# Gathers that add in their buffer: the source rows of an edge-to-node kernel, from group 4 on

## The chip, the cores and the metric

The kernel runs on one core of a Trainium2 chip. The metric is the device time of one launch in microseconds. The kernel before takes 477.14 us, the median of three runs (476.47 to 477.19). A difference of 0.2%, some 0.95 us, is about what a measurement of this kernel can tell from no change.

## The reference

A graph has 50,000 nodes with 128 features each (`x`) and 25,000 edges, sorted by their target. Each edge brings a message, the positive part of its source's row plus its own features. The messages of a node are summed, a two-layer network runs on every node, and a layer norm ends it. All is float32.

```python
msg = relu(x[src] + edge_attr)                     # 25,000 x 128
agg = segment_sum(msg, dst, num_segments=50000)
h = x + agg
h = relu(relu(h @ W1 + b1) @ W2 + b2)              # W1 128x256, W2 256x128
out = layernorm(x + h)                             # over the 128 features, eps 1e-5
```

## The kernel before

The nodes are cut into 131 groups, numbered 0 to 130, of 384 nodes (3 tiles of 128); the last has 80. To each group belongs a window of 256 edges (two chunks of 128), whose start is worked out on the chip from the sorted targets. Groups 0 to 3 are started by hand in halves; from group 4 on every group goes the same way, and the text speaks of those.

The path of the edges of group g:

- SyncE (its queue is SP) loads the edge features of the window into `pre_msg`, slot g % 6 (line 109, 128 KB). `load_ea` first reads the window's start from SBUF into a register, and waits until the slot's last reader, `low_part(g - 6)`, is done.
- GpSimd (POOL) issues two gathers, one for each chunk, each of 128 rows of `x` (64 KB) into `x_src`, slot g % 6 (line 115). They wait for the copy `hT_copied` of group g - 4 (line 559). Behind the gathers of group g POOL normalizes the third tile of group g - 8 (`third_tile`, line 549).
- VectorE (DVE) adds `x_src` to `pre_msg` in place (`add_edge_attr`, line 609), then tells ScalarE by `sum_ready`. It waits for the edge features in the middle of `aggregate` (line 661) and for the gathers just before the addition (line 608).
- ScalarE (ACT) makes the rounded positive part, `high_part` (line 765), VectorE the remainder, `low_part` (line 616), and TensorE adds both to the group's sum by four matmuls with the 0/1 matrix `sel` (line 886).

The path of the nodes: TensorE turns x into the same bank (line 859), ScalarE copies the sum (`hT`, line 771), TensorE and ScalarE run the network (lines 922, 777, 930), VectorE adds bias and x (lines 632, 646) and makes the statistics (653, 662, 668, 673), and ScalarE (796) and POOL (549) write the normalized tiles.

Every engine's order is written out by hand, with semaphores between the engines. In DVE's turn g: add_bias(g), low_part(g+2), add_x(g), reciprocal(g-2), statistics(g), shifts(g-2), select(g+3), aggregate(g), add_edge_attr(g+3). In ACT's turn g high_part(g+2) comes after copy_hT(g+1) and one normalized tile. SyncE's own turn g is what the prediction follows most:

```python
load_x(g + X_AHEAD)      # X_AHEAD = 5; waits for z of group g - 1
load_ea(g + EA_AHEAD)    # EA_AHEAD = 5; waits for low_part of group g - 1
store(g - 4)             # waits for ACT's tiles and for POOL's third_tile(g - 4)
```

SyncE runs these in order, so a store that waits holds up the next loads.

Of the kernel before, what the change touches and what calls it, by code (L numbers as in the profile page):

```python
# [7 lines left out]
ALU = mybir.AluOpType  # L8
# [31 lines left out]
EB, XB, ZB, YB, SB = 6, 6, 8, 6, 8  # L40
# [2 lines left out]
EA_FIRST, EA_AHEAD = 2, 5  # L43

FIRST_CHUNKS = 4
PARTS = {g: [slice(0, 1), slice(1, 2)] for g in range(4)}
WHOLE = {0: 0, 2: 1, 3: 2}
FLAGS = 9
# [2 lines left out]
def partitions(g, c):  # L51
    return LP if g == c["LAST"] else 128


def tiles(g, c):
    return LT if g == c["LAST"] else T


def windows(g, c):
    return 1 if g == c["LAST"] else K  # L60


def parts(g, c):

    return PARTS.get(g, [slice(0, windows(g, c))])


def parts_to(g, c):

    return sum(len(parts(i, c)) for i in range(g))  # L70
# [7 lines left out]
def loads_to(slot, g):  # L78

    return 16 * len(range(slot, g + 1, EB))  # L80


def gathers_to(slot, g, c):

    return 16 * sum(windows(i, c) for i in range(slot, g + 1, EB) if i >= 4)
# [26 lines left out]

def start_gather(nc, x, g, k, loaded, c):
    index = c["last_pairs"][:, 0:1] if g == c["LAST"] else c["src_of"][:, g - FIRST_ROW, k:k + 1]
    nc.gpsimd.indirect_dma_start(  # L115
        out=c["x_src"][:, g % EB, k, :], out_offset=None, in_=x,
        in_offset=bass.IndirectOffsetOnAxis(ap=index, axis=0)).then_inc(loaded, 16)


def start_windows(nc, pairs, c):  # L120
# [45 lines left out]
def prepare(nc, x, edge_attr, dst, pairs, w1, b1, w2, b2, c, sb, sem):  # L166
# [113 lines left out]
    def link(dve, ins):  # L280

        chain[0] += 1
        ins.then_inc(vec, 1)
        dve.wait_ge(vec, chain[0])
# [52 lines left out]
    def prepare_vector(dve):  # L337
# [4 lines left out]
        link(dve, nc.vector.memset(most[:, :], FAR))  # L342
        nc.vector.memset(most[0:1, :], float(FIRST_CHUNKS * EW))

# [47 lines left out]
    def prepare_scalar(act):  # L392
# [4 lines left out]
                      allow_slow_non_contiguous=True).then_inc(next_loaded, 16)  # L397
        act.dma_start(first_pairs[:, 1:FIRST_CHUNKS, :], pairs[EW:FIRST_CHUNKS * EW, :].rearrange("(k p) a -> p k a", p=EW),
                      allow_slow_non_contiguous=True).then_inc(more_pairs_loaded, 16)
# [37 lines left out]
def main_path(nc, x, pairs, edge_attr, out, c, sb, sem, checks):  # L437
# [17 lines left out]
    x_sb, pre_msg, x_loaded, ea_loaded = c["x_sb"], c["pre_msg"], c["x_loaded"], c["ea_loaded"]  # L455

    x_src, sel, end_sel, last_sel = c["x_src"], c["sel"], c["end_sel"], c["last_sel"]
# [14 lines left out]
    xsrc_loaded, sel_ready = c["xsrc_loaded"], c["sel_ready"]  # L472
    out_stored = c["out_stored"]
    targets_ready = sem("targets_ready")
    sum_ready = sem("sum_ready")
# [21 lines left out]
    def inside(g):  # L497

        return 0 <= g < GROUPS
# [44 lines left out]
    def main_gpsimd(pool):  # L544
        def third_tile(g):

            pool.wait_ge(shift_ready, g + 1)
            pool.wait_ge(out_stored[g % YB], (g // YB) * 16)
            nc.gpsimd.tensor_scalar(y[:, g % YB, 2, :], z[:, g % ZB, 2, :], rstd[:, g % SB, 2:3], shift[:, g % SB, 2:3],  # L549
                                    ALU.mult, ALU.add).then_inc(y_tile_ready, 1)  # L550

        pool.wait_ge(c["src_of_ready"], 1)
        for g in (2, 3):
            for k in range(K):
                start_gather(nc, x, g, k, c["first_loaded"][2 * g + k], c)
        for g in range(4, GROUPS):
            back = g - GATHER_AHEAD
            if inside(back):
                pool.wait_ge(hT_copied, back + 1)
            if g == LAST:  # L560
                pool.wait_ge(c["last_pairs_loaded"], 16)
            for k in range(windows(g, c)):
                start_gather(nc, x, g, k, xsrc_loaded[g % EB], c)
            if POOL_FROM <= g - POOL_BACK:
                third_tile(g - POOL_BACK)
        for g in range(GROUPS - POOL_BACK, LAST - 3):
            third_tile(g)

        for g, ts in ((LAST - 3, range(T)), (LAST - 2, (2,)), (END, (1, 2))):
            pool.wait_ge(shift_ready, g + 1)  # L570
            pool.wait_ge(out_stored[g % YB], (g // YB) * 16)
            for t in ts:
                last = nc.gpsimd.tensor_scalar(y[:, g % YB, t, :], z[:, g % ZB, t, :], rstd[:, g % SB, t:t + 1],
                                               shift[:, g % SB, t:t + 1], ALU.mult, ALU.add)
            last.then_inc(y_pool_ready, 1)

    def main_vector(dve):
# [18 lines left out]
        def edge_attr_there(g):  # L596

            dve.wait_ge(ea_loaded[g % EB], loads_to(g % EB, g))

        def add_edge_attr(g, i=0):  # L600

            ks = parts(g, c)[i]
            if g < 4:
                edge_attr_there(g)
            if g < 4:
                dve.wait_ge(c["first_loaded"][2 * g + i], 16 * (ks.stop - ks.start))
            else:
                dve.wait_ge(xsrc_loaded[g % EB], gathers_to(g % EB, g, c))
            nc.vector.tensor_tensor(pre_msg[:, g % EB, ks, :], pre_msg[:, g % EB, ks, :], x_src[:, g % EB, ks, :],  # L609
                                    ALU.add).then_inc(sum_ready, 1)  # L610

# [14 lines left out]
        def add_bias(g):  # L626

            p, n = partitions(g, c), tiles(g, c)
            if g == 0:
                dve.wait_ge(c["b2_loaded"], 16)  # L630
            dve.wait_ge(h2_summed, g + 1)
            nc.vector.tensor_tensor(h2[0:p, g % 2, 0:n, :], h2_ps[g % 2][0:p, 0:n, :], b2_sb[0:p, :, :].to_broadcast([p, n, D]),  # L632
                                    ALU.add).then_inc(h2_ready, 1)
# [22 lines left out]
        def aggregate(g):  # L656
            p = partitions(g, c)
            dve.wait_ge(stats_ready, g + 1)
            for t in range(tiles(g, c)):
                if t == 1 and g >= 1 and inside(g + 3):  # L660
                    edge_attr_there(g + 3)
                last = nc.vector.bn_aggr(mean_var[0:p, g % SB, t, :], stats[0:p, g % SB, t, :])
            last.then_inc(var_ready, 1)

        def reciprocal(g):
            p, n = partitions(g, c), tiles(g, c)
            dve.wait_ge(std_ready, g + 1)
            nc.vector.reciprocal(rstd[0:p, g % SB, 0:n], std[0:p, g % SB, 0:n]).then_inc(rstd_ready, 1)

        def shifts(g):  # L670
            p, n = partitions(g, c), tiles(g, c)
            dve.wait_ge(rstd_ready, g + 1)
            nc.vector.scalar_tensor_tensor(shift[0:p, g % SB, 0:n], mean_var[0:p, g % SB, 0:n, 0], -1.0, rstd[0:p, g % SB, 0:n],  # L673
                                           ALU.mult, ALU.mult).then_inc(shift_ready, 1)
# [40 lines left out]
        statistics(1)  # L715
        select(4)
        aggregate(1)
        add_edge_attr(4)
        for g in range(2, LAST):
            if g == END:  # L720
                for done in (g - 2, g - 1):
                    reciprocal(done)
                    shifts(done)
            add_bias(g)
            if inside(g + 2):
                low_part(g + 2)
            add_x(g)
            if inside(g - 2) and g < END:
                reciprocal(g - 2)
            statistics(g)  # L730
            if inside(g - 2) and g < END:
                shifts(g - 2)
            z_free(g + 1)
            if inside(g + 3):
                select(g + 3)
            aggregate(g)
            if inside(g + 3):
                add_edge_attr(g + 3)
            if g in TARGETS_FOUND:
                checks["find_targets"](dve, TARGETS_FOUND.index(g))  # L740
            if g == TARGETS_CHECKED:
                checks["check_targets"](dve)
            if g == CHECKED + 1:
                checks["set_general"](dve)
# [10 lines left out]
    def main_scalar(act):  # L755
# [5 lines left out]
        def high_part(g, i=0):  # L761

            ks = parts(g, c)[i]
            act.wait_ge(sum_ready, parts_to(g, c) + i + 1)
            nc.scalar.activation(msg_hi[:, g % EB, ks, :], pre_msg[:, g % EB, ks, :], ACT.Relu).then_inc(msg_hi_ready, 1)  # L765

        def copy_hT(g):
# [431 lines left out]
def gnn_resnorm_kernel(nc, x, dst, pairs, edge_attr, w1, b1, w2, b2, out, h_dram):  # L1199
# [9 lines left out]
    with ctx:  # L1209
        def sb(name, shape, dt=FP32):  # L1210
            return ctx.enter_context(nc.sbuf_tensor(name, shape, dt))
# [4 lines left out]
        def sem(name):  # L1216
# [14 lines left out]
            node_row=sb("node_row", [128, K + 1, R]),  # L1231
            first_pairs=sb("first_pairs", [EW, FIRST_CHUNKS, 2], INT32),
            first_dst=sb("first_dst", [EW, FIRST_CHUNKS]),
            last_pairs=sb("last_pairs", [EW, 2], INT32),
# [3 lines left out]
            last_sel=sb("last_sel", [EW, LP], FP32R),  # L1238
            second_sel=sb("second_sel", [EW, FIRST_CHUNKS - 1, T * 128], FP32R),
            first_sel=sb("first_sel", [EW, K, T * 128], FP32R),  # L1240
# [106 lines left out]
```

## Time and profile before

| | us |
|---|---|
| median of 3 runs | 477.14 |
| time of the profiled execution | 474.89 |
| its span, first to last instruction | 473.0 |
| TensorE busy | 457.9 (97% of the span) |
| VectorE busy | 434.3 (92%) |
| ScalarE busy | 395.7 (84%) |
| GpSimd busy | 365.7 (77%) |
| mean granted clock of TensorE, of full speed | 0.993 |

The profiled execution lies 2.25 us under the median. Busy time counts instructions in work, not waits; DMA issues on SyncE don't count. POOL's spans are rough. A releaser named "issue" means that the engine waited for nothing that the profile shows.

### The profile page before, as it was taken

The page shows a single profiled execution, that of the slowest core. Times are in us where ns is not written, and L with a number is a line of the kernel's source. Part 1 is how long each engine was busy: PE and PEld are TensorE (multiplying, and loading weights), DVE is VectorE, ACT ScalarE, POOL GpSimd, SP SyncE. Part 2 cuts the span into 40 slices and gives each one's busy share as a digit, 9 for nine tenths or more (in the row PEclk, how much of TensorE's full clock was granted, in tenths as well). Part 3 has the DMA queues.
Part 4 walks back from the last instruction along what each step waited for, and adds up shares of the span by engine and source line. Part 5 has one row for each costly group of instructions (what it writes and reads, how often), then busy time and mean ns, then how long its engine had stood idle before and what let it go on. Part 6 is the DMA issues. An engine that isn't in the chain of part 4 may idle for free.

```text
span 473.0 us, 10533 instructions
## 1 busy us (share of the span) xinstructions
PE 457.9 (97%) x3033; PEld 378.0 (80%) x3033; DVE 434.3 (92%) x1761; ACT 395.7 (84%) x924; POOL 365.7 (77%) x403
## 2 busy tenths in 40 slices
PE   7879999999999999999999999999999999999994
PEld 5657888888888888888888888888888888888883
DVE  5658999999999999999999999999999999999996
ACT  2349888888888989888988888888889898888885
POOL 6546888888877776787888888888888888888843
PEclk9989999999999999999999999999999999999998
DMA  5625666666667676666666666666666666666632
GB/s 131 178 75 174 185 197 192 197 194 196 195 179 208 180 207 182 209 180 195 192 199 191 196 196 193 199 190 196 194 196 190 200 187 202 186 198 188 198 110 87
DMA packets 83613, 86.80 MB, mean 184 GB/s; under 512 B 11767, under 2 KB 79252, under 8 KB 83556
## 3 DMA queue, kind: packets, MB, share of 16 engines
q1 hardware_dynamic: 74388, 68.76, 46.3%
q0 software_dynamic: 8496, 17.38, 14.2%
q8 instruction: 23, 0.38, 0.4%
q14 instruction: 34, 0.28, 0.2%
q10 hardware_dynamic: 672, 0.00, 0.1%
HBM read 60.51 MB, written 25.60 MB: 182 GB/s over the span
## 4 chain that ended last, share of the span: by engine, by line
PE 95%; DVE 1%; another core or an unknown queue 1%; ACT 1%; issue 0%; DMA 0%; DVEq 0%
PE h_ps L930 37%; PE h1T_ps L922 36%; PE hT_ps L886 12%; PE hT_ps L859 9%; PE h1T_ps L413 1%; DMA dst_first<-in_dst_dram 0%; ACT h1T L777 0%; PE prep_ps L423 0%; ACT hT L771 0%; DVE h L632 0%; DVE stats L653 0%; ACT std L782 0%; DVE z L646 0%; PE prep_ps L912 0%
## 5 line engine op out<-in xcount | busy, mean ns | idle before, releaser
L115 POOL DMA_INDIRECT x_src<-in_x_dram,src_of x256 | 269.4, 1052 | 84.8 <-issue 58.0
L930 PE MATMUL h_ps<-w_sb,h1T 128*128 128x128 f32 x1564 | 197.9, 276 | 1.8 <-issue 1.6
L922 PE MATMUL h1T_ps<-hT,w_sb 128*128 128x384 f32 (+1 forms) x524 | 191.6, 488 | 3.7 <-ACT hT L771 3.7
L777 ACT ACTIVATE h1T<-h1T_ps,b_sb 128x384 f32<-128x384 f32 (+1 forms) x262 | 151.7, 580 | 50.7 <-issue 32.7
L930 PEld LDWEIGHTS h_ps<-w_sb,h1T 128*128 128x128 f32 x1564 | 185.5, 192 | 2.6 <-issue 2.1
L922 PEld LDWEIGHTS h1T_ps<-hT,w_sb 128*128 128x128 f32 x524 | 89.9, 192 | 39.0 <-ACT hT L771 3.5
L796 ACT ACTIVATE y<-z,shift,rstd 128x128 f32<-128x128 f32 x261 | 113.6, 482 | 0.6 <-DVE shift L673 0.5
L632 DVE TENSOR_TENSOR h<-h_ps,b_sb 128x384 f32<-128x384 f32 x131 | 72.7, 555 | 25.6 <-PE h_ps L930 14.7
L549 POOL TENSOR_SCALAR y<-z,rstd,shift 128x128 f32<-128x128 f32 x123 | 85.1, 692 | 13.6 <-DVE shift L673 9.1
L653 DVE BATCH_NORM_STATS2 stats<-z 128x6 f32<-128x128 f32 x391 | 88.7, 282 | 0.1
L859 PEld LDWEIGHTS hT_ps<-ident,x_sb 128*128 128x128 f32 (+1 forms) x379 | 49.5, 142 | 39.6 <-issue 22.8
L592 DVE TENSOR_TENSOR sel<-node_in_range,dst_of 128x432 fp32r<-128x432 f32 x127 | 76.2, 600 | 0.0
L646 DVE SCALAR_TENSOR_TENSOR z<-h,x_sb 128x384 f32<-128x384 f32 x131 | 72.1, 550 | 0.0
L886 PE MATMUL hT_ps<-sel,msg_hi 128*128 128x216 f32 x250 | 71.2, 310 | 0.1
L771 ACT ACTIVATE hT<-hT_ps 128x384 f32<-128x384 f32 x128 | 62.6, 489 | 1.7 <-PE hT_ps L900 1.4
L886 PE MATMUL hT_ps<-sel,msg_lo 128*128 128x216 f32 x250 | 62.3, 276 | 0.0
L859 PE MATMUL hT_ps<-ident,x_sb 128*128 128x128 f32 (+1 forms) x379 | 62.1, 272 | 0.0
L765 ACT ACTIVATE msg_hi<-pre_msg 128x256 fp32r<-128x256 f32 (+1 forms) x132 | 54.3, 412 | 8.6 <-DVE pre_msg L609 4.5
L616 DVE SCALAR_TENSOR_TENSOR msg_lo<-pre_msg,msg_hi 128x256 fp32r<-128x256 f32 (+1 forms) x132 | 54.1, 410 | 4.6 <-ACT msg_hi L765 4.4
L609 DVE TENSOR_TENSOR pre_msg<-pre_msg,x_src 128x256 f32<-128x256 f32 (+1 forms) x135 | 57.7, 428 | 0.4 <-DMA x_src<-in_x_dram,first_pairs 0.4
L886 PEld LDWEIGHTS hT_ps<-sel,msg_hi 128*128 128x128 f32 x250 | 47.7, 191 | 0.4 <-DVE msg_lo L616 0.4
L886 PEld LDWEIGHTS hT_ps<-sel,msg_lo 128*128 128x128 f32 x250 | 48.0, 192 | 0.0
(133 smaller groups left out, 182.8 us busy)
## 6 DMA issues: line engine op xcount, KB each, us to landing
x_sb<-in_x_dram SPq DMA_DIRECT2D x130, 192.0 KB
out_dram<-y SPq DMA_DIRECT2D x130, 192.0 KB
pre_msg<-in_edge_attr_dram SPq DMA_DIRECT2D x130, 128.0 KB
x_src<-in_x_dram,src_of POOLq DMA_INDIRECT x256
w_sb<-in_w_dram SPq DMA_DIRECT2D x2, 128.0 KB
dst_rows<-in_dst_dram SPq DMA_DIRECT2D x1, 97.7 KB
x_src<-in_x_dram,first_pairs POOLq DMA_INDIRECT x4, 2.7
b_sb<-in_b_dram SPq DMA_DIRECT2D x1, 64.0 KB, 3.1
```

The costliest lines, as they stand in the source:

```text
L115: nc.gpsimd.indirect_dma_start(out=c["x_src"][:, g % EB, k, :], out_offset=None, in_=x, in_offset=bass.IndirectOffsetOnAxis(ap=index, axis ...
L549: nc.gpsimd.tensor_scalar(y[:, g % YB, 2, :], z[:, g % ZB, 2, :], rstd[:, g % SB, 2:3], shift[:, g % SB, 2:3], ALU.mult, ALU.add).then_inc ...
L592: nc.vector.tensor_tensor(sel[:, g % EB, :, :], node_in_range[:, :, :].to_broadcast([128, K, T * WP]), dst_of[:, g - FIRST_ROW:g - FIRST_R ...
L632: nc.vector.tensor_tensor(h2[0:p, g % 2, 0:n, :], h2_ps[g % 2][0:p, 0:n, :], b2_sb[0:p, :, :].to_broadcast([p, n, D]), ALU.add).then_inc(h ...
L646: nc.vector.scalar_tensor_tensor(z[0:p, g % ZB, 0:n, :], h2[0:p, g % 2, 0:n, :], 0.0, x_sb[0:p, g % XB, 0:n, :], ALU.max, ALU.add).then_in ...
L653: last = nc.vector.bn_stats(stats[0:p, g % SB, t, :], z[0:p, g % ZB, t, :])
L777: nc.scalar.activation(h1T[:, h, 0:n, 0:p], h1T_ps[h][:, 0:n, 0:p], ACT.Relu, bias=b1_sb[:, h:h + 1]).then_inc(h1_ready, 1)
L796: return nc.scalar.activation(y[0:p, g % YB, t, :], z[0:p, g % ZB, t, :], ACT.Identity, bias=shift[0:p, g % SB, t:t + 1], scale=rstd[0:p, ...
L859: nc.tensor.matmul(sum_bank(g)[:, t, 0:p], x_sb[0:p, g % XB, t, :], ident[0:p, 0:p], is_transpose=True, start=(t == 0), stop=False, skip_g ...
L886: last = nc.tensor.matmul(sum_bank(g)[:, 0:n, p0:p1], part[:, g % EB, k, :], cols, start=False, stop=final, skip_group_check=True)
L922: nc.tensor.matmul(h1T_ps[h][:, 0:n, 0:p], w1_sb[:, h * 128:(h + 1) * 128], hT[:, 0:n, 0:p], start=True, stop=True).then_inc(h1_summed, 1)
L930: last = nc.tensor.matmul(h2_ps[g % 2][0:p, t, :], h1T[:, h, t, 0:p], w2_sb[:, h, :], start=(h == 0 and t == 0), stop=(h == HC - 1), skip_ ...
```

## The change

From group 4 on each gather has `pre_msg`, where the edge features lie, as its destination, and adds to it (`compute_op=ALU.add`). POOL waits for the edge features of group g before it issues the gathers of group g. DVE's additions of groups 4 to 130 go (127 instructions), with their waits for gathers and edge features. ACT's `high_part(g)` waits for the gathers in place of DVE's addition. `x_src` serves the groups 0 to 3 alone.

```diff
+ADDED_FROM = 4
 def start_gather(nc, x, g, k, loaded, c):
     index = ...
-    nc.gpsimd.indirect_dma_start(
-        out=c["x_src"][:, g % EB, k, :], out_offset=None, in_=x,
-        in_offset=bass.IndirectOffsetOnAxis(ap=index, axis=0)).then_inc(loaded, 16)
+    if g < ADDED_FROM:
+        nc.gpsimd.indirect_dma_start(
+            out=c["x_src"][:, g % EB, k, :], out_offset=None, in_=x,
+            in_offset=bass.IndirectOffsetOnAxis(ap=index, axis=0)).then_inc(loaded, 16)
+    else:
+        nc.gpsimd.indirect_dma_start(
+            out=c["pre_msg"][:, g % EB, k, :], out_offset=None, in_=x,
+            in_offset=bass.IndirectOffsetOnAxis(ap=index, axis=0), compute_op=ALU.add).then_inc(loaded, 16)
 # main_gpsimd, in the loop over g from 4
             if g == LAST:
                 pool.wait_ge(c["last_pairs_loaded"], 16)
+            pool.wait_ge(ea_loaded[g % EB], loads_to(g % EB, g))
             for k in range(windows(g, c)):
                 start_gather(nc, x, g, k, xsrc_loaded[g % EB], c)
 # add_edge_attr, now for groups 0 to 3 alone
-            if g < 4:
-                edge_attr_there(g)
-            if g < 4:
-                dve.wait_ge(c["first_loaded"][2 * g + i], 16 * (ks.stop - ks.start))
-            else:
-                dve.wait_ge(xsrc_loaded[g % EB], gathers_to(g % EB, g, c))
+            edge_attr_there(g)
+            dve.wait_ge(c["first_loaded"][2 * g + i], 16 * (ks.stop - ks.start))
 # aggregate
-                if t == 1 and g >= 1 and inside(g + 3):
-                    edge_attr_there(g + 3)
 # DVE's order
-        add_edge_attr(4)
...
-            if inside(g + 3):
-                add_edge_attr(g + 3)
 # high_part
-            act.wait_ge(sum_ready, parts_to(g, c) + i + 1)
+            if g < ADDED_FROM:
+                act.wait_ge(sum_ready, parts_to(g, c) + i + 1)
+            else:
+                act.wait_ge(xsrc_loaded[g % EB], gathers_to(g % EB, g, c))
```

## Rows read from the trace of the kernel before

**Rows 1.** The page: busy us of each engine, its share, its instructions.

```profile
PE 457.9 (97%) x3033; PEld 378.0 (80%) x3033; DVE 434.3 (92%) x1761; ACT 395.7 (84%) x924; POOL 365.7 (77%) x403
```

**Rows 2.** Chain that ended last: shares by engine; pieces (start us, us, what).

```profile
PE 95%; DVE 1%; another core or an unknown queue 1%; ACT 1%; issue 0%; DMA 0%; DVEq 0%
...
55.10 1.35 PE h_ps L930 x12
...
460.85 1.34 PE h_ps L930 x12
```

**Rows 3.** Groups of instructions, 200 to 400 us: count, busy us, mean ns, idle before.

```profile
L609 DVE TENSOR_TENSOR pre_msg<-pre_msg,x_src 128x256 f32<-128x256 f32 x58 | 26.1, 450 | 0.0
```

**Rows 4.** Timeline of POOL, SP's queue and VectorE's z (start us, us, instruction).

```profile
250.01 0.13 SPq L109 DMA_DIRECT2D pre_msg<-in_edge_attr_dram  x1
...
250.70 0.99 POOL L115 DMA_INDIRECT x_src<-in_x_dram,src_of  x1 [0.17 <-issue]
251.99 1.16 POOL L115 DMA_INDIRECT x_src<-in_x_dram,src_of  x1 [0.30 <-issue]
252.36 0.33 SPq L104 DMA_DIRECT2D x_sb<-in_x_dram  x1
253.16 0.39 SPq L109 DMA_DIRECT2D pre_msg<-in_edge_attr_dram  x1
253.19 0.76 POOL L549 TENSOR_SCALAR y<-z,rstd,shift 128x128 f32<-128x128 f32 x1
254.02 0.34 SPq L522 DMA_DIRECT2D out_dram<-y  x1
...
255.19 0.55 DVE L646 SCALAR_TENSOR_TENSOR z<-h,x_sb 128x384 f32<-128x384 f32 x1
...
255.77 0.33 SPq L104 DMA_DIRECT2D x_sb<-in_x_dram  x1
256.81 0.15 SPq L109 DMA_DIRECT2D pre_msg<-in_edge_attr_dram  x1
```

**Rows 5.** Waits of SP's queue: for whom, us in total, times, longest.

```profile
SPq L517 <- POOL y L549: 47.7, 96, 2.5
```

**Rows 6.** Timeline of POOL outside the steady loop.

```profile
15.95 0.96 POOL L115 DMA_INDIRECT x_src<-in_x_dram,src_of  x1 [0.30 <-issue]
50.57 1.27 POOL L115 DMA_INDIRECT x_src<-in_x_dram,src_of  x1 [0.30 <-issue]
457.61 0.45 POOL L549 TENSOR_SCALAR y<-z,rstd,shift 128x128 f32<-128x128 f32 x1 [2.66 <-DVE shift L673]
```

**Rows 7.** DMA by queue, 250.95 to 252.15 us: packets, MB, share of 16 engines.

```profile
q1 hardware_dynamic: 311, 0.21, 58.4%
```

**Rows 8.** DMA packets of 2.10 to 2.20 and of 2.20 to 2.30, then VectorE.

```profile
DMA packets 45, 0.01 MB, mean 58 GB/s; under 512 B 38, under 2 KB 45, under 8 KB 45
...
DMA packets 6, 0.00 MB, mean 48 GB/s; under 512 B 0, under 2 KB 6, under 8 KB 6
...
2.66 0.16 DVE L360 TENSOR_TENSOR first_of<-dst_first,lowest 125x1 f32<-125x1 int32 x1 [0.42 <-DMA dst_first<-in_dst_dram]
```

**Rows 9.** Near the end: gathers, a load, and ACT's high part of group 128.

```profile
446.17 1.16 POOL L115 DMA_INDIRECT x_src<-in_x_dram,src_of  x1 [0.30 <-issue]
447.57 0.16 SPq L109 DMA_DIRECT2D pre_msg<-in_edge_attr_dram  x1
451.69 0.99 POOL L115 DMA_INDIRECT x_src<-in_x_dram,last_pairs  x1 [0.16 <-issue]
455.31 0.42 ACT L765 ACTIVATE msg_hi<-pre_msg 128x256 fp32r<-128x256 f32 x1
```

**Rows 10.** Instructions of tile x_src: from a gather's issue to its landing.

```profile
DMA to landing us min/median/max: 2.7/2.7/2.7
```

**Rows 11.** Stretch 200 to 300 us: clock, DMA share, GB/s; then shares of the queues.

```profile
200.00:300.00 100.00, 100.00 (x674) 82.80 (x673) 95.60 (x381) 88.39 (x206) 83.36 (x89) 1.00 0.64 195
...
q0 software_dynamic: 8496, 17.38, 14.2%
```

## The prediction

> **What bounds the kernel now.** I read four views, in this order. The page gives TensorE 97% and VectorE 92% of the span [rows 1]; the second number tempts one to believe that a VectorE instruction less is time won. The chain of waits says otherwise: 95% of it is TensorE [rows 2], and in it the twelve matmuls of line 930 come back every period with no gap. Their first row here and their last lie 119 periods apart: (460.85 - 55.10) / 119 = 3.41 us for a group [rows 2]. TensorE sets this pace. In it the addition takes 0.45 us of VectorE and nothing waits in front of it [rows 3], so taking it away shortens nothing that TensorE waits for.
>
> Third, the timeline of POOL and of SP's queue over one period. Here the reader is to see how full POOL is: gather 0.99, gap 0.30, gather 1.16, then 0.04, third tile 0.76, gap 0.17 [rows 4]. That is 3.42, the whole period, although the page calls POOL 77% busy. It isn't wholly its own work: apart from the loop a gather takes 0.96 and a third tile 0.45 [rows 6], so with nothing in its way POOL would need some 2.9 us. It has about half a microsecond to spare in each period.
>
> Fourth, the same rows with groups put to them. The last gather, of group 130, starts at 451.69, and 59 periods before it is 250.70, so that gather is of group 71; the load of edge features at 447.57 is of group 129, and 58 periods before it is 250.01, also of group 71 [rows 4, 9]. POOL thus issues the gathers of a group 0.7 us after SP has issued the load of its edge features. Today that is harmless, since they go to different tiles.
>
> **The change part by part.**
>
> *VectorE's additions go.* 127 instructions, 126 of them at about 0.45 us, are some 57 us of VectorE, in 3.41 us periods in which TensorE has no gap. Worth 0 on the path. The removed wait for the edge features costs nothing before (no idle time in front of the addition [rows 3]).
>
> *ACT's high part waits for the gathers.* The second gather of group 128 starts at 446.17 and the high part of that group at 455.31 [rows 9]. A gather lands 2.7 us after its issue [rows 10], so at 448.9: 6.4 us of slack. Costs 0 as long as gathers come no more than 6.4 us later.
>
> *POOL waits for the edge features.* When do they land? From 250.95 to 252.15 the hardware queue moves 311 packets and 0.21 MB [rows 7]. Packets of the edge features have 512 B (256 of them), those of x and of the output 1536 B. With b of the large kind, 311 x 512 + 1024 b = 210,000 gives b = 50, so 261 small ones: within the rounding the whole load, done at 252.15. From the last byte to the waiting engine it takes about 0.46: the small packets of the target numbers end before 2.20 and VectorE, which waits for them, starts at 2.66 [rows 8]. The load is therefore usable at 252.6, L = 2.6 us after its issue at 250.01. From below, 2.15 is the bound (last byte); from above I allow 3.0, since the DMA engines, 64% busy, of which the gathers make 14% [rows 11], get the reads of the destination too. The Trainium skill (page "DMA: Bandwidth & Descriptors", section "Anatomy of one DMA — SWDGE (gpsimd) path") fits a DMA by 2.0 us + bytes / 436e3 per us, which gives an estimate of 2.3 us for 128 KB; this load comes from a hardware queue and the rows show 2.6. With 2.3 the sum below would come out at 3.41 us, that is at no change.
>
> The same page (section "Rules for kernel authors") says that an accumulating DMA reads its destination and writes it later, so that the earlier DMA's semaphore must be waited for. The wait can't be left out, and it speaks against the change: today the gather starts at 250.70, 1.9 us before that semaphore.
>
> *Who stands behind POOL's wait.* On POOL the two gathers and third_tile(g-8). Behind third_tile stands SP: store(g-4) waits for it, and already now this is SP's longest wait, 47.7 us in 96 times [rows 5]. Behind the store in SP's order stand the next load of x and the next load of edge features. So the change closes a loop that is open today: load of edge features g, gathers g, third_tile(g-8), store(g-8), load of x g+1, then load of edge features g+2. It spans two periods, 6.82 us. In numbers of this trace: edge features of 71 at 250.01; third_tile(63) is the POOL row behind the gathers of 71, at 253.19; its store is at 254.02; the x load behind it is at 255.77 and the edge features of 73 at 256.81 [rows 4].
>
> Its length once closed:
> - L, 2.6 us;
> - two gathers, 2 G, and 0.30 + 0.04 between and behind them;
> - third tile, 0.60, between the 0.45 alone and the 0.76 in the loop [rows 4, 6];
> - until the store starts 0.07 (253.95 to 254.02), the store's issue 0.34, some 0.04 to the next, the issue of x 0.33 [rows 4];
> - from there to the issue of edge features 0.60: the rows show 0.47 (252.69 to 253.16) and 0.71 (256.10 to 256.81) [rows 4].
>
> Together L + 2 G + 2.32. The wait for z in front of the x load (z ends at 255.74, the load starts at 255.77 [rows 4]) drops out when SP is later than that.
>
> *What a gather that adds costs POOL (G).* The trace has no such gather. From below: 0.96, a gather alone [rows 6], since the count of rows and the index column stay. I see no reason for less. From above the nearest row is the longest kind, 1.27 [rows 6], and with no row for the second source of each row (the destination has to be read), twice that of today, 1.9, isn't excluded. I take 1.10, near the rows of the plain gathers, with something for the second read.
>
> *Sum.* Loop = 2.6 + 2.2 + 2.32 = 7.12, so 3.56 us a group, 0.15 over TensorE's 3.41. POOL alone would be at 2.2 + 0.30 + 0.04 + 0.60 + 0.17 = 3.31, under the period, so the loop decides. It exists from group 12 on (the first with a third tile), 118 turns: 118 x 0.15 = 17.8 us. Of that the slack hides a part: the wait puts the gathers 1.9 us later at once, 6.4 - 1.9 = 4.5 us are left to be eaten before TensorE waits. 17.8 - 4.5 = 13.3 us. The profiled execution would go from 474.89 to 488.2; set on the median of 477.14, it is 490.4. I say 490.
>
> *Start and end.* The 1% of the chain that belongs to "another core or an unknown queue" [rows 2] is released by nothing that the change touches; 0. At the end no load follows, so nothing new.
>
> **The rivals.**
>
> *The loop stays shorter than the period.* It needs L + 2 G under 4.5: G = 0.96 and L = 2.5, say, that is 6.74 us or 3.37 a group. Even 0.047 us a group over is hidden but for 1 us (118 x 0.047 - 4.5 = 1.0). For it: G may be as today, POOL no longer meets the addition on VectorE, and L has its lower bound at 2.15. Then TensorE stays at 3.41 and the time at 477. A loop of 6.91 us is the turning point.
>
> *POOL becomes the bound by the making of the gather itself.* Its own period is 2 G + 1.11, the loop's half is G + 2.46; from G = 1.35 on POOL is the longer one. At G = 1.45 it has 4.01: 118 x 0.60 - 4.5 = 66, so 543 us; at 1.6, 4.31, it would be 579. For it: a gather that adds names two sources for each row. Against it: nothing in this trace shows that the duration goes by the number of rows rather than by the instruction.
>
> *Faster.* The only mechanism is at the start, where VectorE's first additions of large groups precede the high parts by little; a microsecond at most, 476 us. TensorE's back-to-back chain speaks against more.
>
> *The change doesn't do what it says*, that is, the addition is made in another way than by the DMA engines, for instance by POOL itself: that is G far above, the second rival's place.
>
> **How the numbers follow.** Loop over the period with G under 1.35, the forecast: 0.45, 490 us, alone from 478 to 522 (G = 1.35 and L = 2.6: 3.81 a group, 118 x 0.40 - 4.5 = 43). Loop under the turning point: 0.28, 477. POOL bound: 0.21, 520 to 580 and more. Faster by over 0.2%: 0.06, 476. So slower 0.66, same 0.28, faster 0.06. The range goes from 475.5 to 540: it takes in the same case, the forecast and the lower part of POOL's, and leaves out about 0.12 above and a few hundredths below. 0.2%, 0.95 us, is about what can be measured here.
>
> **What the changed profile would show.** POOL's gathers with idle time in front of them, released by the DMA of the edge features. The gathers of a group some 2.6 us behind its load in place of 0.7. SP's wait for the third tile longer, its wait for z gone. The gaps of TensorE in front of line 886, with VectorE's low part, ACT's high part and the gathers behind them. A chain that leaves TensorE for POOL, SP and DMA. If TensorE's row stays at 3.41 us a group, the loop is shorter than I sum it; if POOL's gaps vanish and the gathers last over 1.35 us, it is POOL. I would be wrong above all by G, of which 0.1 us is worth 118 x 0.1 = 12 us, and by L, of which 0.1 us is worth 6 us.

## The result: 614.6 us, 29% slower

| | before | after |
|---|---|---|
| median us | 477.16 | 614.62 (613.18 to 616.67) |
| ratio | | 1.289 (95% interval 1.285 to 1.293) |
| span of the profiled execution | 473.0 | 612.5 |
| TensorE busy, share of the span | 97% | 80% |
| POOL busy, share of the span | 77% | 80% |

The direction was forecast; the size, 137 us, lies far outside the range of 475.5 to 540. First the page of the changed kernel: busy us of each engine, DMA queues, and the chain that ended last.

```profile
PE 488.9 (80%) x3033; PEld 381.8 (62%) x3033; DVE 407.4 (67%) x1634; ACT 383.1 (63%) x924; POOL 487.9 (80%) x403
...
DMA packets 111949, 86.80 MB, mean 142 GB/s; under 512 B 11767, under 2 KB 111636, under 8 KB 111892
...
q0 software_dynamic: 36832, 17.38, 23.1%
...
issue 33%; POOL 28%; DMA 18%; SPq 6%; ACT 6%; PE 5%; DVE 4%; ACTq 0%; POOLq 0%; DVEq 0%
...
L121 POOL DMA_INDIRECT pre_msg<-in_x_dram,src_of x252 | 400.3, 1589 | 107.1 <-issue 65.7
```

TensorE has left the chain: 5% in place of 95% [rows 2]. VectorE did lose its 127 instructions (1,634 in place of 1,761 [rows 1]), and got nothing for it. A gather takes POOL 1.59 us. The bytes of the software queue, nearly all of them the gathers', are as before, 17.38 MB [rows 11], but they come in 36,832 packets, against 8,496.

The waits of the changed kernel: who waited for whom, us in total, times, the longest.

```profile
ACT msg_hi L766 <- DMA pre_msg<-in_x_dram,src_of: 175.9, 117, 2.8
DVE msg_lo L619 <- ACT msg_hi L766: 167.0, 110, 3.0
PEld hT_ps L887 <- DVE msg_lo L619: 117.4, 87, 2.6
...
POOL pre_msg L121 <- DMA pre_msg<-in_edge_attr_dram: 41.4, 48, 1.2
```

Read from below: POOL waits for the edge features in 48 groups, some two of five, ACT waits for the gathers in 117, and that wait runs through VectorE to TensorE. Now the closed loop itself, in the timeline of POOL and SP's queue. (A third tile's row starts before the gather in front of it ends; what counts is its end.)

```profile
298.13 0.39 SPq L110 DMA_DIRECT2D pre_msg<-in_edge_attr_dram  x1
...
301.74 1.57 POOL L121 DMA_INDIRECT pre_msg<-in_x_dram,src_of  x1 [1.19 <-DMA pre_msg<-in_edge_attr_dram]
303.62 1.54 POOL L121 DMA_INDIRECT pre_msg<-in_x_dram,src_of  x1 [0.30 <-issue]
304.62 1.05 POOL L555 TENSOR_SCALAR y<-z,rstd,shift 128x128 f32<-128x128 f32 x1
305.75 0.34 SPq L528 DMA_DIRECT2D out_dram<-y  x1
305.84 1.58 POOL L121 DMA_INDIRECT pre_msg<-in_x_dram,src_of  x1 [0.17 <-issue]
306.14 0.43 SPq L105 DMA_DIRECT2D x_sb<-in_x_dram  x1
307.40 0.40 SPq L110 DMA_DIRECT2D pre_msg<-in_edge_attr_dram  x1
```

From one load of edge features (298.13) to the second next (307.40) are 9.27 us, 4.64 a group; over 99 groups the first gathers lie 4.62 us apart. That is the loop that the prediction named. There is another reading of the same rows: from 301.74 to 305.84 POOL worked without a wait, 4.10 us for one group, also far over 3.41. So two bounds may lie over each other, the loop and POOL's own work, and the experiments take them apart.

### The profile page after: what moved, and what is told of

The parts are those of the page before. It is cut to its first block, busy times and chain, and to the rows that moved or that the text cites. A ratio compares the mean times of both kernels' runs of the same rounds, so it can differ in the third digit from the quotient of the medians.

```text
span 612.5 us, 10532 instructions
## 1 busy us (share of the span) xinstructions
PE 488.9 (80%) x3033; PEld 381.8 (62%) x3033; DVE 407.4 (67%) x1634; ACT 383.1 (63%) x924; POOL 487.9 (80%) x403
## 3 DMA queue, kind: packets, MB, share of 16 engines
q0 software_dynamic: 36832, 17.38, 23.1%
## 4 chain that ended last, share of the span: by engine, by line
issue 33%; POOL 28%; DMA 18%; SPq 6%; ACT 6%; PE 5%; DVE 4%; ACTq 0%; POOLq 0%; DVEq 0%
POOL pre_msg L121 23%; DMA pre_msg<-in_edge_attr_dram 13%; POOL y L555 4%; DMA pre_msg<-in_x_dram,src_of 4%; ACT y L797 3%; SPq L105 2%; SPq L97 2%; SPq L528 2%; PE hT_ps L887 1%; ACT msg_hi L766 1%; DVE msg_lo L619 1%; PE h_ps L931 1%; PE h1T_ps L923 1%; ACT hT L772 1%; DVE stats L656 1%
## 5 line engine op out<-in xcount | busy, mean ns | idle before, releaser
L121 POOL DMA_INDIRECT pre_msg<-in_x_dram,src_of x252 | 400.3, 1589 | 107.1 <-issue 65.7
L619 DVE SCALAR_TENSOR_TENSOR msg_lo<-pre_msg,msg_hi 128x256 fp32r<-128x256 f32 (+1 forms) x132 | 56.0, 425 | 176.6 <-ACT msg_hi L766 167.0
L887 PE MATMUL hT_ps<-sel,msg_hi 128*128 128x216 f32 x250 | 73.7, 320 | 108.9 <-DVE msg_lo L619 94.9
L778 ACT ACTIVATE h1T<-h1T_ps,b_sb 128x384 f32<-128x384 f32 (+1 forms) x262 | 137.2, 568 | 9.6 <-PE h1T_ps L923 5.1
L555 POOL TENSOR_SCALAR y<-z,rstd,shift 128x128 f32<-128x128 f32 x123 | 138.0, 1145 | 2.3 <-DVE shift L674 2.3
L797 ACT ACTIVATE y<-z,shift,rstd 128x128 f32<-128x128 f32 x261 | 114.9, 486 | 9.2 <-DVE shift L674 2.6
L887 PEld LDWEIGHTS hT_ps<-sel,msg_lo 128*128 128x128 f32 x250 | 47.7, 191 | 0.0
L663 DVE BATCH_NORM_AGGREGATE mean_var<-stats 128x2 f32<-128x6 f32 x391 | 39.6, 154 | 0.2
```

The source lines that it names most:

```text
L121: nc.gpsimd.indirect_dma_start(out=c["pre_msg"][:, g % EB, k, :], out_offset=None, in_=x, in_offset=bass.IndirectOffsetOnAxis(ap=index, ax ...
L778: nc.scalar.activation(h1T[:, h, 0:n, 0:p], h1T_ps[h][:, 0:n, 0:p], ACT.Relu, bias=b1_sb[:, h:h + 1]).then_inc(h1_ready, 1)
L797: return nc.scalar.activation(y[0:p, g % YB, t, :], z[0:p, g % ZB, t, :], ACT.Identity, bias=shift[0:p, g % SB, t:t + 1], scale=rstd[0:p, ...
L887: last = nc.tensor.matmul(sum_bank(g)[:, 0:n, p0:p1], part[:, g % EB, k, :], cols, start=False, stop=final, skip_group_check=True)
```

## The experiments

The median of before was 475.2 us beside the first four kernels, 476.9 beside the next four, 475.7 beside the last three.

**The wait alone.** Gathers plain, VectorE adds, POOL waits for the edge features.

```diff
             if g == LAST:
                 pool.wait_ge(c["last_pairs_loaded"], 16)
+            pool.wait_ge(ea_loaded[g % EB], loads_to(g % EB, g))
             for k in range(windows(g, c)):
```

> The kernel before, plus POOL's wait for the edge features before the gathers of groups 4 to 130; the gathers stay plain and VectorE adds. Theory (the loop load of edge features, two gathers, third tile, store, next loads is real, but only long gathers and a late landing make it longer than two periods): with plain gathers it is L + 2 G + 2.32 = 2.6 + 1.98 + 2.32 = 6.9 us, 3.45 a group, of which the slack of 4.5 us hides all: 475 to 482 us, gathers 2.6 us behind the issue of their load. Rival (the wait itself is what costs, whatever the gathers): 540 us or more.

Measured: 547.1 us, ratio 1.149 (1.145 to 1.153). One added wait costs 72 us. My theory's 475 to 482 us were far off; the rival's 540 or more came. The timeline of this kernel, POOL and SP's queue:

```profile
303.21 0.39 SPq L109 DMA_DIRECT2D pre_msg<-in_edge_attr_dram  x1
...
306.50 1.04 POOL L115 DMA_INDIRECT x_src<-in_x_dram,src_of  x1 [1.35 <-DMA pre_msg<-in_edge_attr_dram]
307.85 1.10 POOL L115 DMA_INDIRECT x_src<-in_x_dram,src_of  x1 [0.30 <-issue]
308.99 0.75 POOL L549 TENSOR_SCALAR y<-z,rstd,shift 128x128 f32<-128x128 f32 x1
309.81 0.34 SPq L522 DMA_DIRECT2D out_dram<-y  x1
310.20 0.42 SPq L104 DMA_DIRECT2D x_sb<-in_x_dram  x1
311.36 0.39 SPq L109 DMA_DIRECT2D pre_msg<-in_edge_attr_dram  x1
```

The loop is 311.36 - 303.21 = 8.15 us, 4.07 a group, where I had summed 6.9. Its largest term is 3.29 from the issue of the load to POOL's start; in the 53 groups in which POOL waited for it the median is 3.3. I had 2.6. Over 99 groups the first gathers lie 4.07 us apart, and 118 x (4.07 - 3.41) - 4.5 = 73 us: the prediction's way from the loop to the time fits here.

**The addition in the gathers alone.** They add, but into `x_src`, which is cleared once at the start, and don't wait; VectorE adds as before. Old rows stay in the sums.

```diff
     nc.gpsimd.indirect_dma_start(
         out=c["x_src"][:, g % EB, k, :], out_offset=None, in_=x,
-        in_offset=bass.IndirectOffsetOnAxis(ap=index, axis=0)).then_inc(loaded, 16)
+        in_offset=bass.IndirectOffsetOnAxis(ap=index, axis=0),
+        **(dict(compute_op=ALU.add) if g >= 4 else {})).then_inc(loaded, 16)
```

> The kernel before with gathers that add, but into x_src (cleared once, so old rows stay in the sums), and with no wait for the edge features; VectorE's addition stays. Theory (the making of a gather that adds takes POOL 1.58 us): POOL's own period is 2 x 1.58 + 0.30 + 0.5 + 0.17 = 4.1 us, so 118 x 0.7 - 6 = 77 over before: 545 to 560 us, POOL without waits. Rival (the wait is the cost, POOL's longer instruction only shows the DMA engines or a lock held elsewhere): 477 to 485 us. A second rival (all of the loss is from the gathers, on the DMA engines or on POOL): 610 us here too.

Measured: 589.7 us, ratio 1.242 (1.240 to 1.244), 30 us above the top of what I expected. The chain of this kernel by engine:

```profile
POOL 70%; issue 26%; DVE 1%; DMA 1%; PE 1%; ACT 0%; DVEq 0%; POOLq 0%; ACTq 0%
```

And what POOL waited for (us in total, times, the longest):

```profile
POOL x_src L115 <- issue: 62.3, 256, 0.3
```

POOL never waits, the 0.3 us between two of its instructions apart, and is the chain. So POOL's own work is a bound without any wait. Over 99 groups its first gathers lie 4.40 us apart, where I had summed 4.1: the two gathers with their gap take 3.57 in the mean, for 3.46, and the third tile behind them 0.66, for 0.5. The two parts don't add up: 72 and 114 us alone, 137 together.

**The addition taken away from VectorE alone.** The messages are made of the edge features only.

```diff
-        add_edge_attr(4)
...
-            if inside(g + 3):
-                add_edge_attr(g + 3)
# high_part, from group 4 on
+                act.wait_ge(ea_loaded[g % EB], loads_to(g % EB, g))
+                act.wait_ge(xsrc_loaded[g % EB], gathers_to(g % EB, g, c))
```

> The kernel before without VectorE's additions of groups 4 to 130 (messages are then made of the edge features alone); plain gathers into x_src, ACT's high part waits for edge features and gathers. What it is worth to take the addition from VectorE if nothing else changes. Theory (TensorE sets the pace with no gap): 477 us, within 1.5. Rival (VectorE at 92% is near enough to the bound that its relief shows): 465 us or less.

Measured: 476.2 us, ratio 1.002 (1.001 to 1.003). Its page, busy us by engine:

```profile
PE 457.8 (97%) x3033; PEld 377.9 (80%) x3033; DVE 391.2 (83%) x1634; ACT 382.9 (81%) x924; POOL 354.4 (75%) x403
```

VectorE is 43 us less busy and TensorE as busy as before [rows 1]. The relief of VectorE, with nothing else changed, is worth nothing.

**What an adding gather costs POOL.** Other forms of gather by stretch of groups, into `pre_msg`; parts of the sums are left out.

```diff
+        adds, p, n = form(g)      # groups 4: add 128 rows; 30: plain 128; 50: add 64; 70: plain 64;
+                                  # 90: add 128 rows of 256 B; 110: add 32 rows
         nc.gpsimd.indirect_dma_start(
-            out=c["pre_msg"][:, g % EB, k, :], out_offset=None, in_=x,
-            in_offset=bass.IndirectOffsetOnAxis(ap=index, axis=0), compute_op=ALU.add).then_inc(loaded, 16)
+            out=c["pre_msg"][0:p, g % EB, k, 0:n], out_offset=None, in_=x.rearrange("r (h d) -> (r h) d", d=n),
+            in_offset=bass.IndirectOffsetOnAxis(ap=index[0:p, :], axis=0),
+            **(dict(compute_op=ALU.add) if adds else {})).then_inc(loaded, 16)
```

> The changed kernel with other gathers by stretch of groups, into pre_msg (parts of the sums are left out): 4 to 29 add 128 rows, 30 to 49 plain 128 rows, 50 to 69 add 64 rows, 70 to 89 plain 64 rows, 90 to 109 add 128 rows of 256 B, 110 to 130 add 32 rows. Theory (POOL writes descriptors one by one, a gather that adds has a second source for each row): duration = a + b x rows, with b about twice as large for adding: plain 0.95 at 128 rows and less at 64, adding 1.57 at 128, some 1.1 at 64, 0.9 at 32, and 1.57 for 128 rows of 256 B. Rival (the longer gather waits for the DMA engines, which read and write more bytes): 256 B rows take clearly less than 512 B rows. Rival (a fixed extra for an adding gather, whatever the rows): 1.57 at 64 and 32 rows too.

The kernel ran once, in 578.8 us; what counts here are its rows. The gathers in one window of each of the six stretches, in their order (80 to 120 us, 160 to 220, 240 to 300, 330 to 370, 410 to 460, 500 to 540): count, busy us, mean ns.

```profile
L122 POOL DMA_INDIRECT pre_msg<-in_x_dram,src_of x18 | 28.9, 1604 | 7.7 <-issue 6.3 <-DMA pre_msg<-in_edge_attr_dram 1.4
...
L122 POOL DMA_INDIRECT pre_msg<-in_x_dram,src_of x31 | 31.5, 1017 | 20.7 <-DMA pre_msg<-in_edge_attr_dram 14.0 <-issue 6.7
...
L122 POOL DMA_INDIRECT pre_msg<-in_x_dram,src_of x27 | 40.2, 1487 | 14.3 <-issue 9.0 <-DMA pre_msg<-in_edge_attr_dram 5.1 <-ACT hT L783 0.2
...
L122 POOL DMA_INDIRECT pre_msg<-in_x_dram,src_of x20 | 19.3, 966 | 12.7 <-DMA pre_msg<-in_edge_attr_dram 8.1 <-issue 4.6
...
L122 POOL DMA_INDIRECT pre_msg<-in_x_dram,src_of x23 | 37.7, 1638 | 8.4 <-issue 7.3 <-ACT hT L783 1.1
...
L122 POOL DMA_INDIRECT pre_msg<-in_x_dram,src_of x19 | 27.1, 1427 | 8.2 <-issue 5.6 <-DMA pre_msg<-in_edge_attr_dram 1.5 <-ACT hT L783 1.1
```

The second window runs into the next stretch: two of its 31 gathers already add (those at 217.36 and 219.15). The 29 plain ones from 160 to 216 us have a mean of 0.98. So 128 rows take 1.60 us adding and 0.98 plain, 64 rows 1.49 and 0.97, 32 rows 1.43 adding; half as many bytes a row save nothing (1.64). My theory, a cost by the row, twice as large for adding, fell. Of the 0.62 us that adding costs at 128 rows, 0.52 are still there at 64. So most of the extra goes neither by the rows nor by the bytes; that it is paid for each instruction is tested further below.

**The third tile first.** The changed kernel, with the order of POOL turned.

```diff
+            if POOL_FROM <= g - POOL_BACK:
+                third_tile(g - POOL_BACK)
             pool.wait_ge(ea_loaded[g % EB], loads_to(g % EB, g))
             for k in range(windows(g, c)):
                 start_gather(nc, x, g, k, xsrc_loaded[g % EB], c)
-            if POOL_FROM <= g - POOL_BACK:
-                third_tile(g - POOL_BACK)
```

> The changed kernel with POOL's third_tile(g - 8) ahead of the wait and the gathers of group g, so that the store of g - 8 no longer hangs on the gathers of g. Theory (two bounds lie over each other in the changed kernel: the closed loop, 9.2 us in two periods, 4.6 a group, and POOL's own work, 4.1 to 4.4 a group): the loop opens and POOL's own work is left, 475 + 118 x (4.1 to 4.4 - 3.41) - 6 = 551 to 586 us, POOL without waits for the edge features. Rival (it is POOL alone; the loop only shows): 612 us or more, no gain. Rival (it is the loop alone): below 530.

**The features early.** The changed kernel, with more slots.

```diff
-EB, XB, ZB, YB, SB = 6, 6, 8, 6, 8
+EB, XB, ZB, YB, SB = 8, 6, 8, 6, 8
-EA_FIRST, EA_AHEAD = 2, 5
+EA_FIRST, EA_AHEAD = 2, 7
...
         load_x(4)
+        load_ea(5)
+        load_ea(6)
```

> The changed kernel with eight slots in place of six, and the edge features loaded seven groups ahead in place of five: the wait stays, but what it waits for is there long before. Theory: as with the tile first, POOL's own work is left, 551 to 586 us, no idle time of POOL for the edge features. Rival (the late landing isn't needed for the loss): 612 us. Rival (the loop alone): below 530.

Measured: 583.4 us (ratio 1.224, 1.219 to 1.229) and 582.5 (1.223, 1.219 to 1.228), both inside the 551 to 586 expected. Two ways to open the loop give the same time, and nearly that of the adding gathers alone, whose pace is 0.05 us a group slower, with VectorE's addition still beside it; why, I didn't test. Two POOL rows of the kernel with the tile first, one period apart:

```profile
301.03 1.59 POOL L121 DMA_INDIRECT pre_msg<-in_x_dram,src_of  x1 [0.17 <-issue]
...
305.42 1.57 POOL L121 DMA_INDIRECT pre_msg<-in_x_dram,src_of  x1 [0.17 <-issue]
```

And POOL's line among its waits:

```profile
POOL pre_msg L121 <- issue: 60.3, 250, 0.3
```

They are 4.39 us apart; over 99 groups the mean is 4.35 here and 4.34 in the other kernel. In the one shown POOL doesn't wait for the features in the steady loop. So POOL's own work accounts for 583 - 477 = 106 us of the loss, and the loop, which is longer still, for the other 31.

**The wait alone, third tile first.** The same turn of order as above, in the kernel with plain gathers.

> The kernel with the wait alone (plain gathers, VectorE adds; 547 us), and POOL's third tile ahead of wait and gathers. Theory (all of the wait's price is the closed loop through the store): 475 to 479 us, as the kernel before. Rival (the price is the later landing of the gathers at VectorE's addition): 530 us or more.

Measured: 480.7 us (475.6 to 483.2), ratio 1.011 (1.006 to 1.016). Of 72 us some 67 are gone. Nearly all of the wait's price is the closed loop through the store. What is left, about 1%, I didn't follow up; the profiled execution, 475.6, is the fastest and doesn't show it.

**The wait alone, features ahead of x in SP's turn.**

```diff
         for g in range(GROUPS):
-            if inside(g + X_AHEAD):
-                load_x(g + X_AHEAD)
             if inside(g + EA_AHEAD):
                 load_ea(g + EA_AHEAD)
+            if inside(g + X_AHEAD):
+                load_x(g + X_AHEAD)
             if inside(g - 4):
```

> The kernel with the wait alone (547 us, loop 8.1 us in two periods), and in SP's turn the load of the edge features ahead of that of x. Theory (the load lands 3.3 us after its issue and not 2.6 since, once the loop is closed, store, x load and edge features are issued within 1.6 us and the 384 KB in front go first): the issue of x (0.42) and its data (0.6) leave the loop, 7.1 us, 3.55 a group: 475 + 118 x 0.14 - 4.5 = 487 us, 478 to 500; the edge features usable some 2.7 us after their issue. Rival (3.3 us have another cause): only the issue leaves, 7.7 us, 3.85 a group: 522 us.

Measured: 505.0 us, ratio 1.062 (1.057 to 1.066). It lies between the theory's 487 and the rival's 522; neither came. The time from issue to POOL's start did not fall: its median, over the 29 groups in which POOL waited, is 3.5 us. So the load of x in front isn't what makes it 3.3, and that theory fell. It isn't excluded for the store, which still stands in front, and nearer. The gain came from SP. From the start of a store to that of the load of features it was 1.55 us (309.81 to 311.36 above); here, in SP's rows, it is 0.82:

```profile
302.83 0.34 SPq L522 DMA_DIRECT2D out_dram<-y  x1
303.65 0.39 SPq L109 DMA_DIRECT2D pre_msg<-in_edge_attr_dram  x1
```

The loop of 8.15 less 0.73 is 7.42, 3.71 a group; the first gathers lie 3.69 us apart.

**Half the features, the wait alone.** To tell data from fixed time in those 3.3 us. The second chunk's features are left out.

```diff
-    n = windows(g, c)
+    n = windows(g, c) if g < 6 else 1
     sp.dma_start(c["pre_msg"][:, g % EB, 0:n, :],
```

> The kernel with the wait alone (547 us), and from group 6 on only the first chunk of the edge features is loaded (64 KB in place of 128; the second chunk's features are left out). Tells what makes up the 3.3 us from the issue of the load to POOL's start. Theory (its data take 0.9 us, the rest is fixed, with 1.2 us between the last byte and POOL's start): L falls by 0.45 to 2.9, the loop from 8.1 to 7.7, 3.85 a group, 475 + 118 x 0.44 - 4.5 = 522 us, 510 to 530. Rival (it goes by the bytes): L 1.7, the loop opens, 477.

Measured: 537.0 us, ratio 1.126 (1.120 to 1.132), outside my 510 to 530. With half the bytes the median from issue to POOL's start is 3.15 us in 44 groups, against 3.3: 0.2 less, not 0.45. Most of it doesn't go by the bytes. The kernel with the whole load shows where it goes: these are its DMA packets by queue from 304.20 to 305.30 and from 305.30 to 305.90 us, behind the issue at 303.21.

```profile
DMA packets 297, 0.20 MB, mean 179 GB/s; under 512 B 26, under 2 KB 282, under 8 KB 296
q1 hardware_dynamic: 271, 0.13, 41.8%
...
DMA packets 16, 0.01 MB, mean 14 GB/s; under 512 B 14, under 2 KB 14, under 8 KB 16
q0 software_dynamic: 15, 0.01, 4.5%
```

0.13 MB in 271 packets is the load of 256 rows. The first 1.0 us behind the issue brings nearly nothing of it, the data take 1.1. Behind 305.3 the hardware queue is all but empty, and POOL starts at 306.50, 1.2 us behind the last byte. What fills these 1.2 us stays open, and so does why half the bytes save 0.2 and not half of the 1.1.

**The third tile on VectorE.** The changed kernel; the third tile of groups 4 to 126 goes to VectorE, and POOL only gathers.

```diff
# POOL
             for k in range(windows(g, c)):
                 start_gather(nc, x, g, k, xsrc_loaded[g % EB], c)
-            if POOL_FROM <= g - POOL_BACK:
-                third_tile(g - POOL_BACK)
-        for g in range(GROUPS - POOL_BACK, LAST - 3):
-            third_tile(g)
# VectorE
             aggregate(g)
+            if POOL_FROM <= g - 3:
+                normal_tile(g - 3, 2).then_inc(y_tile_ready, 1)
```

> The changed kernel with the third tile of groups 4 to 126 on VectorE, in the place of the removed addition; POOL only gathers, and no store waits for POOL. Theory (POOL's time for two adding gathers is the floor): 1.58 + 0.30 + 1.58 + 0.30 = 3.76 us a group, 475 + 118 x 0.35 - 6 = 510 us, 504 to 517. Rival (the DMA engines, which move an adding gather in packets of one row, hold POOL back): 560 us or more. Rival (the third tile was the cost, the gathers are covered): 477.

Measured: 510.1 us, ratio 1.074 (1.071 to 1.077). This one came as summed. POOL's timeline shows its bound most plainly, gather behind gather, 1.54 + 0.30:

```profile
300.40 1.54 POOL L121 DMA_INDIRECT pre_msg<-in_x_dram,src_of  x1 [0.30 <-issue]
302.24 1.54 POOL L121 DMA_INDIRECT pre_msg<-in_x_dram,src_of  x1 [0.30 <-issue]
304.09 1.54 POOL L121 DMA_INDIRECT pre_msg<-in_x_dram,src_of  x1 [0.30 <-issue]
```

Two of them are 3.69 us; over 99 groups the first gathers lie 3.72 us apart, over the 3.41 of TensorE. Even with POOL's third tile taken away the change can't be had for nothing.

**One gather of two adds.** The kernel with wait and tile first; the first chunk's gather adds, VectorE adds the second chunk.

```diff
+    adds = k == 0 and 4 <= g < c["LAST"]
     nc.gpsimd.indirect_dma_start(
-        out=c["x_src"][:, g % EB, k, :], out_offset=None, in_=x,
-        in_offset=bass.IndirectOffsetOnAxis(ap=index, axis=0)).then_inc(loaded, 16)
+        out=c["pre_msg" if adds else "x_src"][:, g % EB, k, :], out_offset=None, in_=x,
+        in_offset=bass.IndirectOffsetOnAxis(ap=index, axis=0),
+        **(dict(compute_op=ALU.add) if adds else {})).then_inc(loaded, 16)
...
# add_edge_attr, from group 4 on
+                ks = slice(1, 2) if g < LAST else ks
```

> The kernel with wait and third tile first (481 us), and of each group's two gathers only the first adds; VectorE adds the second chunk alone. Theory (each adding gather costs POOL a fixed extra of its own): POOL 1.60 + 0.30 + 1.05 + 0.04 + 0.6 + 0.17 = 3.76 us a group, 475 + 118 x 0.35 - 6 = 510 us, 500 to 530. Rival (the price is paid once a group, not per gather): 583 us. Rival (one adding gather still fits into POOL's spare time): 481.

Measured: 522.9 us, ratio 1.102 (1.098 to 1.106), inside my 500 to 530 though over the 510. The chain of this kernel by engine:

```profile
POOL 50%; issue 29%; PE 9%; DMA 6%; DVE 4%; ACT 1%; SPq 0%; POOLq 0%; ACTq 0%; DVEq 0%
```

Its first gathers lie 3.80 us apart over 99 groups. With half the adding gathers it is 42 us over the kernel it was made from, where POOL's own work with both costs 106. A price paid once a group would have given 583: it is paid for each gather that adds. One of the two already takes POOL past TensorE's pace.

No experiment points to a version faster than the kernel before. TensorE's gapless 3.41 us a group are the bound there [rows 2], and no experiment shortens them.

## Why the prediction was wrong

*What bounds the kernel before*: right. With VectorE's additions gone and nothing else changed, the time stays.

*The closed loop*: right in its way, SP's order and POOL's, and in its form. It is twice 4.64 us. Term by term, with the rows of the changed kernel shown above (one turn; the mean of 111 is 9.25):

| term | predicted | measured |
|---|---|---|
| L, issue of the features to POOL's start | 2.6 | 3.61 |
| two gathers and the gap between | 2.5 | 3.42 |
| what the third tile adds behind them | 0.64 | 0.51 |
| to the store's start, and on to the x load | 0.45 | 0.47 |
| x load to the load of features | 0.93 | 1.26 |
| loop | 7.12 | 9.27 |

Put into my own last step this gives 118 x (4.62 - 3.41) - 4.5 = 138 us, and 137 were measured. The step from loop to time held. The steps that failed are the sizes of two terms: what a gather that adds costs POOL, G, taken as 1.10 us and measured as 1.58, and the time from the load's issue to POOL's start, L, taken as 2.6 and measured as 3.6. They make the loop longer by 0.92 and 1.01 us, of 2.15 in all; SP's way from the x load to the load of features adds 0.33.

*L*. I took the time from the last byte to the waiting engine from the start of the kernel, 0.46 us [rows 8]. That row is of the start, with small packets, 58 GB/s on the DMA engines against 195 in the steady loop [rows 8, 11], and VectorE waiting. In the steady loop, with plain gathers, it is 1.2 us, while the last byte came 2.1 us behind the issue, as read. 3.0 was my upper bound; 3.3 is the median with plain gathers and 3.6 with adding ones. In the first experiment's expectation I kept 2.6, since I put the 3.6 of the changed kernel down to its gathers. There it is 0.7 of the 1.25 us that my sum of 6.9 missed; the rest lies in the gathers (2.45 with their gap, for 2.28), the third tile (0.79 for 0.64) and the way from the x load to the features (1.16 for 0.93).

*G*. I took 1.10 and it is 1.58, in a range that I myself had drawn to 1.9. The value was taken near the end that the trace showed, where it showed nothing of the kind asked for. "With no row for the second source" was a reason for the middle of that range, not for its foot. My own upper end of 1.9 put into the rival's formula gives 118 x (4.91 - 3.41) - 4.5 = 172 us, some 650; the range ended at 540, which is G = 1.44, and so left out the upper half of what I had called possible. The rival in which POOL becomes the bound had 0.21; for G = 1.6 it said 579 us, and with the loop opened 583 were measured. In the changed kernel itself the loop bounds: it is longer than POOL's own work by 0.27 us a group (4.62 against 4.35). So the turning point that I had put at G = 1.35 isn't one here: with the longer L the loop stays ahead of POOL.

*Slack*: 4.5 us hidden once fits the sum above and that of the wait alone; no run changes the slack by itself. *VectorE's relief*: worth nothing, as forecast. *The changed profile*: idle time before POOL's gathers released by the DMA, the gathers some 3.5 us behind their load and not 2.6, ACT waiting for the gathers, the chain gone from TensorE: seen. SP's wait for the third tile grew from 47.7 us [rows 5] to 314.4, and its wait for z fell from 23.9 to 9.4. That POOL's gaps would vanish if POOL were the bound was seen only with the loop open.

The two rules of the Trainium skill that I weighed (page "DMA: Bandwidth & Descriptors"): its section "Anatomy of one DMA — SWDGE (gpsimd) path" gives a fit for a DMA issued by GpSimd, and by it an estimate of 2.3 us for this load, which comes from SP's queue, and so no change; the runs show 3.3 and 3.6, and the measurement decides. Its section "Rules for kernel authors" asks for the wait, and here the runs put a price on it: 72 us where the gathers stand ahead of the tile that the store needs, about 5 where they don't.

## What to carry to other kernels

Before adding a wait to an in-order engine, follow what stands behind it round to the thing it waits for: a wait that closes a circle costs its whole length each turn, and moving one independent instruction ahead of it may open the circle again. An engine with hardly any idle time before its instructions may have little left to give, whatever its busy share says: POOL was 77% busy here and had half a microsecond of 3.41 to spare. While no row shows what a longer instruction costs, the range of the forecast must reach as far as that of its cost. And a latency is better read where the load is, from a wait of the same engine, than from the quiet start of the kernel.

## What the runs showed of the hardware

- A gather of 128 rows of 512 B that adds into SBUF takes POOL 1.54 us at least, a plain one 0.94. The extra changes little with the rows (0.62 us in the mean for 128 rows, 0.52 for 64; 32 rows adding take 1.43) and not with the bytes of a row (1.64 for 256 B).
- With adding gathers the software queue's 17.38 MB go in 36,832 packets, with plain ones in 8,496, and its packets take 23.1% of the 16 engines' 612.5 us, 141 us, against 67 (14.2% of 473.0). The DMA engines weren't the bound for it: with the tile on VectorE the pace, 3.72 us, was POOL's two gathers and gaps, 3.69, to within 0.03 us.
- A 128 KB load from SP's queue let POOL go on 3.3 us after its issue began (median of 53 waits; in the one looked at closely 1.2 of them lay behind its last packet), and a 64 KB load 3.15 us (44 waits). With adding gathers in flight it was 3.6.
